# Low halves of the node tiles and of the first weight on GpSimd, transposes by DMA, in a two-layer graph network kernel

## The chip, the core and the metric

The kernel runs on one core of one Trainium2 chip. The metric is the device time of one execution in microseconds. Before the change the median of three runs is 846.42 us (845.54 to 846.95).

## What is computed

1250 nodes with 768 features and 41250 edges (sorted by destination, self loops among them). A graph convolution with a residual and a layer norm comes first, then two attention layers, then a last norm:

```
edge_index = jnp.stack([src, dst])
x = _layernorm(x + _L0_gnn_ref(x, edge_index, L0_gnn_W, L0_gnn_b), axis=-1)
x = _layernorm(x + _L1_gnn_ref(x, edge_index, ...), axis=-1)

def _L0_gnn_ref(x, edge_index, W, b):
    ...
    deg = jax.ops.segment_sum(jnp.ones_like(dst, dtype=x.dtype), dst, num_segments=n)
    norm = deg_inv_sqrt[src] * deg_inv_sqrt[dst]
    h = x @ W
    msg = h[src] * norm[:, None]
    out = jax.ops.segment_sum(msg, dst, num_segments=n)
    return out + b
```

The change touches only how `h = x @ W` of the first layer gets its operands.

## The kernel before

**Tiles and stages.** Nodes lie in T = 10 tiles of 128, features in KD = 6 pieces of 128. Every engine has its own program with semaphores by name; nothing is planned at run time but the number of loop rounds. The stages follow each other: keys of the edges (to about 18 us), counting (to about 129 us), aggregation of the first layer, then the attention layers. The change lies in the counting stage.

**Counting.** The adjacency matrix is built as counts, in NB = 80 blocks of 16 destination nodes. For a block VectorE makes one-hot matrices of six edge tiles (`one_hots`, L1376 for the low part of the source, L1377 for the key) in one of four ring slots; TensorE multiplies them (`count_block`, six matmuls at L819) into one of three PSUM slots, after `open_block` (L806) has begun the slot with the self loops. ScalarE (ACT) copies a finished block out twice (L1113, and L1114, which appears as L1078, the line of its helper `cast`) and gives the slot back with `blk_free`. Every eight blocks VectorE shifts the keys (L1396) and takes low counts (L1385), and TensorE sums degrees (L830).

**The node product between the blocks.** f32 products are made of f16 halves: high times high, low times high, high times low (`node_parts`, L764, two matmuls of 512 and 256 columns for each). Behind block b the function `first_nodes` (b below 18) does pieces of node tiles 0 and 1: in blocks 0 to 5 those that need no low weight, in blocks 6 to 11 it waits for `w_lo` of piece b - 6. From block 18 on, 43 of the 62 blocks carry one piece of tiles 2 to 9 (`project_nodes`); tile 2 begins at block 19, tile 3 at 28, and each later one some nine blocks on. The last five pieces come behind the blocks.

**How the operands are made.** Tile t of x lies in SBUF in f32. TensorE transposes its six pieces (`transposes`, L725) into PSUM; ACT casts them to the high half (`xt_high`), VectorE subtracts that from PSUM for the low half (`xt_low`, L1355). For tiles 2 to 9 this happens at the blocks of FETCH: 13, 19, 28, 37, 45, 54, 63 and 71 (VectorE four blocks later). Of the first weight ACT casts 64 times the rows (`weights`, through L1078) and VectorE makes the low half in one instruction (L1275), one behind each odd block below 12.

**Queues.** SP loads edges, x and the weight at the start, and then waits for the whole node product (`h_done`). GpSimd makes constants until about 8 us and then waits for the last block.

**What GpSimd and VectorE do elsewhere, where the rows below come from.** GpSimd multiplies by a constant (L610 of 128 elements, L640 of 1024), copies (L652), subtracts (L658), and takes a power of one element a partition for the norms: at L636 VectorE waits for it before L1450, at L672 VectorE goes on with L1615, an operation of two SBUF inputs.

Of the kernel before, what the change touches and what calls it, by code (L numbers as in the profile page):

```python
# [17 lines left out]
P = 128  # L18
# [31 lines left out]
FETCH_LAG = 4  # L50
# [10 lines left out]
def done_block(t):  # L61

    return next(b for b in range(NB) if pieces_until(b) >= (t + 1) * KD)


FETCH = {done_block(t) + 2: t + 2 for t in range(T - 2)}
# [56 lines left out]
def gnn_program(nc, x, src, dst, W0, b0, W1, a_src1, a_dst1, b1, g1, be1, Wr1, br1,  # L123
# [7 lines left out]
    with ExitStack() as ctx:  # L131
# [103 lines left out]
        w0_lo = at(195 * KB, [KD, D], f16)  # L235
        src_i = at(156 * KB, [EG, P], i32)
# [119 lines left out]
        def everywhere(row):  # L356
# [7 lines left out]
            x_in0 x_in1 x_in2 x_in3 x_in4 x_in5 x_in6 x_in7 x_in8 x_in9 x_tr xt_hi_ok xt_lo_ok h_done h_read hs_hi_ok hs_lo_ok  # L364
# [65 lines left out]
        def _(sp):  # L430
# [18 lines left out]
            for t in range(T):  # L449
                if t == 2:  # L450
                    weights(0)
                if t < T - 1:
                    sp.dma_start(x_sb[:, t, :], x[t * P:(t + 1) * P, :]).then_inc(S[f"x_in{t}"], 16)
                else:
                    sp.wait_ge(S["pads"], 3)
                    sp.dma_start(x_sb[0:LAST, t, :], x[t * P:N, :]).then_inc(S[f"x_in{t}"], 16)
            sp.wait_ge(S["h_done"], T)
# [130 lines left out]
        def _(pool):  # L588
# [30 lines left out]

            def param(name, row, slot, n=HC):  # L620
                pool.dma_start(par_rows[:, slot, 0:n], everywhere(row)).then_inc(S[name], 16)
# [76 lines left out]
        def _(pe):  # L698
# [18 lines left out]
            def transposes(t):  # L717

                pe.wait_ge(S[f"x_in{t}"], 16)
                if t >= 2:  # L720
                    pe.wait_ge(S["h_read"], t - 1)
                else:
                    pe.wait_ge(S["ident_ok"], 4)
                for k in range(KD):
                    last = pe.transpose(p_out[t % 2][:, k * P:(k + 1) * P], x_sb[:, t, k * P:(k + 1) * P], ident)  # L725
                last.then_inc(S["x_tr"], 1)
# [63 lines left out]
            def project_nodes(t, k, counted=False):  # L790

                if k == 0:
                    pe.wait_ge(S["xt_lo_ok"], t + 1)
                last = node_parts(t, k, NODE_PARTS, counted)
                if k == KD - 1:
                    last.then_inc(S["h_done"], 1)
# [43 lines left out]
            for b in range(NB):  # L840
# [12 lines left out]
                if b in FETCH:  # L853
                    transposes(FETCH[b])
# [221 lines left out]
        def _(act):  # L1076
            def cast(out_, in_, signal, scale=1.0):
                act.activation(out_, in_, ACT.Copy, scale=scale).then_inc(signal, 1)  # L1078
# [8 lines left out]
            def xt_high(t):  # L1087

                act.wait_ge(S["x_tr"], t + 1 if t < 2 else t + 3)
                cast(xt_hi[:, :, t * P:(t + 1) * P], p_out[t % 2].rearrange("p (k n) -> p k n", k=KD), S["xt_hi_ok"])  # L1090

# [5 lines left out]
            def node_evict(t):  # L1097

                act.wait_ge(S["h_done"], t + 1)
                cast(h_sb[:, t, :], p_out[t % 2], S["h_read"], 1 / WSCALE)  # L1100
# [8 lines left out]
            for b in range(NB):  # L1109
# [5 lines left out]
                if b in FETCH:  # L1115
                    xt_high(FETCH[b])
# [149 lines left out]
        def _(dve):  # L1266
# [84 lines left out]
            def xt_low(t):  # L1351

                dve.wait_ge(S["xt_hi_ok"], t + 1)
                cols = slice(t * P, (t + 1) * P)
                dve.tensor_tensor(xt_lo[:, :, cols], p_out[t % 2].rearrange("p (k n) -> p k n", k=KD), xt_hi[:, :, cols],  # L1355
                                  ALU.subtract).then_inc(S["xt_lo_ok"], 1)

# [29 lines left out]
            for b in range(NB):  # L1387
# [4 lines left out]
                if b % 2 == 1 and b < 2 * KD:  # L1392
                    weights(0, [b // 2])
# [3 lines left out]
                if b - FETCH_LAG in FETCH:  # L1397
                    xt_low(FETCH[b - FETCH_LAG])
# [463 lines left out]
```

## Time and profile before

| | |
|---|---|
| median of the runs | 846.42 us |
| the profiled execution, its own time | 845.6 us |
| its span, first to last instruction | 843.8 us |
| TensorE matmul (PE) busy | 810.1 us, 96% of the span |
| VectorE (DVE) busy | 671.5 us, 80% |
| ScalarE (ACT) busy | 269.1 us, 32% |
| GpSimd (POOL) busy | 59.6 us, 7% |
| granted clock of TensorE, mean | 0.994 |

Busy time says how full an engine is, not who sets the pace: that is read from the chain that ended last and from the idle time before each group of instructions. Spans of GpSimd are rough. Matmuls overlap, so the pace of TensorE is read from start to start.

### The profile page before, as it was taken

Reading aid. Unit: us, or ns where it says so; the run is one execution under the profiler, and the core shown is the slowest. Engines: PE = TensorE matmul, PEld = TensorE weight load, DVE = VectorE, ACT = ScalarE, POOL = GpSimd, SP = SyncE. Lnnn points to the kernel's source line nnn. Section 1 sums busy time; section 2 is a strip of 40 time slices with the busy share of each in tenths; the row PEclk is TensorE's granted clock in tenths of the full one; section 3 lists DMA queues with packets and bytes.
Section 4 is the critical chain, followed back from the end, with each engine's and each line's share of the span. In section 5 each row is a group of like instructions: output and inputs, shape, how many; then the busy total and the mean of one; then the engine's idle time right before and its main releaser. Section 6 shows DMA issues by size and latency. Waiting matters only on the chain.

```text
span 843.8 us, 13751 instructions
## 1 busy us (share of the span) xinstructions
PE 810.1 (96%) x5022; PEld 535.6 (63%) x5022; DVE 671.5 (80%) x1181; ACT 269.1 (32%) x510; POOL 59.6 (7%) x81
## 2 busy tenths in 40 slices
PE   5899998999999999999999998999999999999995
PEld 4577774665554444447888887886666666655553
DVE  7999985777566659999988889969873197996686
ACT  3544446010011201015555455643301107760000
POOL 3000002011003000000000000011110000001111
PEclk9999999999999999999999999999999999999998
DMA  8000004041132343226112104113213342212232
GB/s 308 4 2 2 2 3 169 25 162 57 45 156 69 100 163 140 82 104 216 52 68 82 56 1 137 57 63 125 88 64 94 120 134 75 71 57 75 75 113 71
DMA packets 24588, 73.55 MB, mean 87 GB/s; under 512 B 2756, under 2 KB 3756, under 8 KB 24398
## 3 DMA queue, kind: packets, MB, share of 16 engines
q1 hardware_dynamic: 23262, 67.61, 23.0%
q0 software_dynamic: 1264, 5.11, 1.8%
q8 instruction: 39, 0.64, 0.3%
q14 instruction: 23, 0.19, 0.1%
HBM read 52.40 MB, written 20.31 MB: 86 GB/s over the span
## 4 chain that ended last, share of the span: by engine, by line
PE 80%; DVE 11%; issue 3%; DMA 2%; DVEq 2%; ACT 1%; SPq 0%; POOL 0%; POOLq 0%
PE psum L963 19%; PE psum L990 19%; PE psum L1071 12%; PE psum L752 10%; PE psum L878 8%; DVE arena L1463 6%; PE psum L764 6%; PE psum L819 3%; PE psum L978 1%; PE psum L1004 1%; DVEq L1365 1%; PE psum L915 1%; DMA arena<-as_scratch 1%; ACT arena L1078 1%; PE psum L725 1%
## 5 line engine op out<-in xcount | busy, mean ns | idle before, releaser
L990 PE MATMUL psum<-arena 128*128 128x257 f32 x800 | 175.4, 381 | 3.0 <-DVE arena L1607 2.0
L1078 ACT ACTIVATE arena<-psum 128x160 f16<-128x160 f32 (+6 forms) x188 | 94.0, 528 | 261.8 <-PE psum L752 74.0
L990 PEld LDWEIGHTS psum<-arena 128*128 128x128 f32 x800 | 151.2, 190 | 26.7 <-ACT arena L1078 2.7
L752 PE MATMUL psum<-arena 128*128 128x512 f16 x720 | 161.0, 382 | 2.4 <-DVE arena L1435 2.1
L963 PE MATMUL psum<-arena 128*128 128x512 f16 x960 | 158.5, 326 | 0.2 <-ACT arena L1078 0.2
L963 PEld LDWEIGHTS psum<-arena 128*128 128x128 f16 x960 | 93.5, 98 | 62.3 <-ACT arena L1078 0.5
L752 PEld LDWEIGHTS psum<-arena 128*128 128x128 f16 x720 | 70.6, 99 | 85.8 <-issue 5.1
L1071 PE MATMUL psum<-arena 128*128 128x512 f16 (+2 forms) x600 | 98.4, 326 | 0.0
L1071 PEld LDWEIGHTS psum<-arena 128*128 128x128 f16 x600 | 58.3, 97 | 39.8
L1463 DVE CUSTOM_DVE_ANT_0 arena<-arena 128x1280 bf16<-128x1280 bf16 x50 | 71.0, 1488 | 14.3 <-DMA arena<-as_scratch 8.5
L1181 ACT ACTIVATE arena<-arena 128x640 f32<-128x640 f32 x80 | 64.6, 836 | 50.1 <-DVE arena L1592 49.7
L1607 DVE SCALAR_TENSOR_TENSOR arena<-arena 128x640 f32<-128x640 f32 x80 | 65.4, 819 | 15.2 <-ACT arena L1181 9.2
L1078 ACT ACTIVATE arena<-arena 128x768 f16<-128x768 f32 (+4 forms) x58 | 45.7, 809 | 88.4 <-DMA arena<-in_L_gnn_Wr_dram 43.7
L1592 DVE SCALAR_TENSOR_TENSOR arena<-arena 128x640 f32<-128x640 f32 x80 | 70.1, 878 | 0.6 <-DMA arena<-uv_scratch 0.6
L878 PE MATMUL psum<-arena 128*128 128x512 f16 (+1 forms) x400 | 66.7, 326 | 2.7 <-DVE arena L1418 1.9
L764 PE MATMUL psum<-arena 128*128 128x512 f16 x360 | 68.5, 325 | 0.1
L878 PEld LDWEIGHTS psum<-arena 128*128 x400 | 38.3, 98 | 30.8 <-issue 6.2
L1377 DVE TENSOR_TENSOR arena<-arena 128x960 f16<-128x960 int16 x80 | 52.7, 659 | 0.0
L819 PE MATMUL psum<-arena 128*128 128x160 f16 x480 | 46.5, 233 | 3.4 <-DVE arena L1377 2.9
L1376 DVE TENSOR_TENSOR arena<-arena 128x768 f16<-128x768 int16 x80 | 44.7, 559 | 2.0 <-PEq L837 1.2
L819 PEld LDWEIGHTS psum<-arena 128*128 128x128 f16 x480 | 36.5, 97 | 13.6 <-DVE arena L1377 6.9
L1473 DVE CUSTOM_DVE_ANT_0 arena<-psum,arena 128x256 bf16<-128x256 f32 x80 | 28.3, 421 | 20.9 <-PE psum L752 20.9
(173 smaller groups left out, 713.7 us busy)
## 6 DMA issues: line engine op xcount, KB each, us to landing
arena<-in_L_gnn_W_dram SPq DMA_DIRECT2D x22, 384.0 KB, 3.4
r_scratch<-arena SPq DMA_DIRECT2D x10, 512.0 KB, 2.6
arena<-uv_scratch SPq DMA_DIRECT2D x16, 320.0 KB, 4.3
arena<-r_scratch SPq DMA_DIRECT2D x10, 512.0 KB, 3.7
x_scratch<-arena SPq DMA_DIRECT2D x10, 384.0 KB, 4.5
arena<-x_scratch SPq DMA_DIRECT2D x10, 384.0 KB, 3.5
r_scratch<-arena SPq DMA_DIRECT2D x10, 384.0 KB, 2.6
arena<-r_scratch SPq DMA_DIRECT2D x10, 384.0 KB, 3.8
```

Of the source, the lines that this page charges most:

```text
L752: ins = pe.matmul(o[:, a:b], part[:, k, ds(t * P, P)], w[:, k, a:b], start=(not begun and k == 0 and n == 0 and m == 0), stop=(k == kn - 1 ...
L764: last = pe.matmul(p_out[t % 2][:, a:b], part[:, k, t * P:(t + 1) * P], w[:, k, a:b], start=(k == 0 and name == "hh"), stop=(k == KD - 1 a ...
L819: last = pe.matmul(o, ring_lo[slot][:, i // 2, :, i % 2], ring_key[slot][:, i // 2, :, i % 2], start=False, stop=False, skip_group_check=True)
L878: ins = pe.matmul(p_out[par][:, a:b], counts, part[:, k, a:b], start=(not low and k == 0 and n == 0), stop=(not low and k == T - 1 and n = ...
L963: ins = pe.matmul(o[:, a:b], part[:, k, :], w[k][:, a:b], start=(k == 0 and n == 0 and m == 0), stop=(k == KH - 1 and n == 1))
L990: last = pe.matmul(p_att[:, ATT_BANKS[ch][j], 0:HID + 1], pf[n % PSLOTS][:, j * P:(j + 1) * P], xl[ch % H][:, k, 0:HID + 1], start=(k == 0 ...
L1071: last = pe.matmul(p_att2[c % 2][:, j, a:b], p[n][:, t % C1 * P:(t % C1 + 1) * P], xl2[:, k, a:b], start=(k == 0 and m == 0), stop=(k == T ...
L1078: act.activation(out_, in_, ACT.Copy, scale=scale).then_inc(signal, 1)
L1181: act.activation(ee[s], ee[s], ACT.Exp, bias=as_s[:, ch % H, k:k + 1]).then_inc(S["ex_ok"], 1)
L1463: dve.tensor_tensor_reduce(out=out_, in0=mask, in1=row, scale=1.0, scalar=NEG_BIG, op0=ALU.add, op1=ALU.max, accum_out=mx[:, col, t:t + 1] ...
L1592: dve.scalar_tensor_tensor(ee[s], u_row, asd[:, ch % H, k:k + 1], v_row, ALU.add, ALU.max).then_inc(S["larger_ok"], 1)
L1607: dve.scalar_tensor_tensor(pf[n % PSLOTS], ee[s], 1.0, CT[:, k, ds(ch // H * W1C, W1C)], ALU.min, ALU.mult).then_inc(S["pf_ok"], 1)
```

## The change

ACT casts tiles 2 to 9 to their high halves in SBUF, not yet transposed (`x_high`, at blocks 2, 5, 8, ... 23, into one of three slots). GpSimd subtracts for the low halves, also in SBUF. SP issues a DMA transpose for each half of each tile into `xt_hi` and `xt_lo`. GpSimd also makes the low halves of the first weight, in two instructions a row: it multiplies the row by 64 in place, then subtracts the high half. TensorE's transposes and VectorE's subtractions for these tiles, and VectorE's low halves of the first weight, go. New waits: ACT's `x_high` from tile 5 on waits until both halves of tile t - 3 have landed, GpSimd's steps wait for the casts, SP's transposes for GpSimd and ACT, `project_nodes` for the landings and for the eviction of tile t - 2.

```diff
--- before.py
+++ after.py
@@ -47,7 +47,6 @@
 TAIL = 1
 PACK = 10
 HELD = 5
-FETCH_LAG = 4
 HS_FIRST = 3
 
 
@@ -63,7 +62,8 @@
     return next(b for b in range(NB) if pieces_until(b) >= (t + 1) * KD)
 
 
-FETCH = {done_block(t) + 2: t + 2 for t in range(T - 2)}
+SPLIT_X = {2 + 3 * i: i + 2 for i in range(T - 2)}
+XSLOTS = 3
 G_SHIFT = 18
 G_INVERSE = -(-2 ** G_SHIFT // G)
 EG = -(-ET // P)
@@ -233,6 +233,8 @@
         xt_lo = at(110 * KB, [KD, NP], f16)
         w0_hi = at(186 * KB, [KD, D], f16)
         w0_lo = at(195 * KB, [KD, D], f16)
+        x_hi = [at((177 + 3 * i) * KB, [D], f16) for i in range(XSLOTS)]
+        x_lo = [at((177 + 3 * i) * KB + 1536, [D], f16) for i in range(XSLOTS)]
         src_i = at(156 * KB, [EG, P], i32)
         dst_i = at(156 * KB + 1536, [EG, P], i32)
         hi_i = at(159 * KB, [EG, P], i32)
@@ -361,7 +363,7 @@
         S = {n: sem(n) for n in """
             pads src_in dst_in iotas ident_ok keys_prep keys_tr tile_rows ranges_f ranges_t ranges_i key_shift
             keys_ready0 keys_ready1 keys_ready2 keys_ready3 keys_free0 keys_free1 keys_free2 keys_free3 blk_done blk_free
-            x_in0 x_in1 x_in2 x_in3 x_in4 x_in5 x_in6 x_in7 x_in8 x_in9 x_tr xt_hi_ok xt_lo_ok h_done h_read hs_hi_ok hs_lo_ok
+            x_in0 x_in1 x_in2 x_in3 x_in4 x_in5 x_in6 x_in7 x_in8 x_in9 x_tr xt_hi_ok xt_lo_ok x_hi_ok x_lo_ok xt_in0 xt_in1 w_scaled h_done h_read hs_hi_ok hs_lo_ok
             w_in0 w_in1 w_in2 w_in3 w_in4 w_in5 w_hi w_lo clo_ok deg_done dinv_ok over_ok flag_done flag_ok
             neg_tr neg_ok gcn_done gcn_read gcn_var gcn_rstd x1_ok x1_out
             x1_tr x1t_hi_ok x1t_lo_ok as_ok as_tr as_rows as_dram asr0 asr1 max_ok
@@ -454,6 +456,13 @@
                 else:
                     sp.wait_ge(S["pads"], 3)
                     sp.dma_start(x_sb[0:LAST, t, :], x[t * P:N, :]).then_inc(S[f"x_in{t}"], 16)
+            for t in range(2, T):
+                if t >= 4:
+                    sp.wait_ge(S[f"xt_in{t % 2}"], 32 * (t // 2 - 1))
+                for half, made in ((xt_hi, "x_hi_ok"), (xt_lo, "x_lo_ok")):
+                    sp.wait_ge(S[made], t - 1)
+                    sp.dma_start_transpose(half[:, :, t * P:(t + 1) * P],
+                                           (x_hi if half is xt_hi else x_lo)[t % XSLOTS]).then_inc(S[f"xt_in{t % 2}"], 16)
             sp.wait_ge(S["h_done"], T)
             weights(1)
             for t in range(T):
@@ -617,6 +626,17 @@
             pool.tensor_scalar(not_first, ident[:, 0:1], -1.0, None, ALU.add).then_inc(S["br1_ok"], 1)
             pool.memset(half, -0.5).then_inc(S["half_ok"], 1)
 
+            for k in range(KD):
+                pool.wait_ge(S[f"w_in{k}"], 16)
+                pool.wait_ge(S["w_hi"], k + 1)
+                pool.tensor_scalar(wst0[k], wst0[k], WSCALE, None, ALU.mult).then_inc(S["w_scaled"], 1)
+                pool.wait_ge(S["w_scaled"], k + 1)
+                pool.tensor_tensor(w0_lo[:, k, :], wst0[k], w0_hi[:, k, :], ALU.subtract).then_inc(S["w_lo"], 1)
+            for t in range(2, T):
+                pool.wait_ge(S[f"x_in{t}"], 16)
+                pool.wait_ge(S["x_hi_ok"], t - 1)
+                pool.tensor_tensor(x_lo[t % XSLOTS], x_sb[:, t, :], x_hi[t % XSLOTS], ALU.subtract).then_inc(S["x_lo_ok"], 1)
+
             def param(name, row, slot, n=HC):
                 pool.dma_start(par_rows[:, slot, 0:n], everywhere(row)).then_inc(S[name], 16)
 
@@ -717,10 +737,7 @@
             def transposes(t):
 
                 pe.wait_ge(S[f"x_in{t}"], 16)
-                if t >= 2:
-                    pe.wait_ge(S["h_read"], t - 1)
-                else:
-                    pe.wait_ge(S["ident_ok"], 4)
+                pe.wait_ge(S["ident_ok"], 4)
                 for k in range(KD):
                     last = pe.transpose(p_out[t % 2][:, k * P:(k + 1) * P], x_sb[:, t, k * P:(k + 1) * P], ident)
                 last.then_inc(S["x_tr"], 1)
@@ -790,7 +807,8 @@
             def project_nodes(t, k, counted=False):
 
                 if k == 0:
-                    pe.wait_ge(S["xt_lo_ok"], t + 1)
+                    pe.wait_ge(S["h_read"], t - 1)
+                    pe.wait_ge(S[f"xt_in{t % 2}"], 32 * (t // 2))
                 last = node_parts(t, k, NODE_PARTS, counted)
                 if k == KD - 1:
                     last.then_inc(S["h_done"], 1)
@@ -850,8 +868,6 @@
                     for q in range(pieces_until(b - 1), pieces_until(b)):
                         project_nodes(q // KD, q % KD, counted)
                         counted = False
-                if b in FETCH:
-                    transposes(FETCH[b])
                 assert not counted
                 if j == SUBS - 1 and 1 <= t <= T - TAIL:
                     degrees(t - 1)
@@ -1086,8 +1102,15 @@
 
             def xt_high(t):
 
-                act.wait_ge(S["x_tr"], t + 1 if t < 2 else t + 3)
+                act.wait_ge(S["x_tr"], t + 1)
                 cast(xt_hi[:, :, t * P:(t + 1) * P], p_out[t % 2].rearrange("p (k n) -> p k n", k=KD), S["xt_hi_ok"])
+
+            def x_high(t):
+
+                act.wait_ge(S[f"x_in{t}"], 16)
+                if t - XSLOTS >= 2:
+                    act.wait_ge(S[f"xt_in{(t - XSLOTS) % 2}"], 32 * ((t - XSLOTS) // 2))
+                cast(x_hi[t % XSLOTS], x_sb[:, t, :], S["x_hi_ok"])
 
             def xt_rest(t):
 
@@ -1096,6 +1119,10 @@
 
             def node_evict(t):
 
+                if t == T - XSLOTS:
+                    act.wait_ge(S["x_lo_ok"], T - 2)
+                    for i in range(2):
+                        act.wait_ge(S[f"xt_in{i}"], 32 * (T // 2 - 1))
                 act.wait_ge(S["h_done"], t + 1)
                 cast(h_sb[:, t, :], p_out[t % 2], S["h_read"], 1 / WSCALE)
 
@@ -1112,8 +1139,8 @@
                 counted = p_c[b % CSLOTS].rearrange("p (k j) -> p k j", k=T)
                 act.activation(CT[:, :, b * WD:(b + 1) * WD], counted, ACT.Copy)
                 cast(c_hi[:, :, b * WD:(b + 1) * WD], counted, S["blk_free"])
-                if b in FETCH:
-                    xt_high(FETCH[b])
+                if b in SPLIT_X:
+                    x_high(SPLIT_X[b])
                 for n in range(T - 1):
                     if done_block(n) == b:
                         node_evict(n)
@@ -1348,13 +1375,6 @@
             dve.wait_ge(S["dve"], steps_done(1))
             dve.scalar_tensor_tensor(packed, g_tiles, float(1 << PACK), first_up, ALU.mult, ALU.add).then_inc(S["ranges_i"], 1)
 
-            def xt_low(t):
-
-                dve.wait_ge(S["xt_hi_ok"], t + 1)
-                cols = slice(t * P, (t + 1) * P)
-                dve.tensor_tensor(xt_lo[:, :, cols], p_out[t % 2].rearrange("p (k n) -> p k n", k=KD), xt_hi[:, :, cols],
-                                  ALU.subtract).then_inc(S["xt_lo_ok"], 1)
-
             dve.wait_ge(S["dve"], steps_done())
             dve.wait_ge(S["ranges_i"], 1)
             r0, r1 = dve.alloc_register("dve_first"), dve.alloc_register("dve_end")
@@ -1389,13 +1409,9 @@
                 if t and j == 0:
                     dve.wait_ge(S["key_shift"], t)
                 one_hots(b)
-                if b % 2 == 1 and b < 2 * KD:
-                    weights(0, [b // 2])
                 if j == SUBS // 2 and t + 1 < T:
                     dve.wait_ge(S["blk_done"], t * SUBS)
                     dve.tensor_scalar(key_s[(t + 1) % 2], key_s[t % 2], float(-P), None, ALU.add).then_inc(S["key_shift"], 1)
-                if b - FETCH_LAG in FETCH:
-                    xt_low(FETCH[b - FETCH_LAG])
                 if j == SUBS // 2 + 2 and 1 <= t <= T - TAIL:
                     low_counts(t - 1)
             for t in range(T - TAIL, T):
```

## Rows read from the trace of the kernel before

**Rows 1.** The page, part 4: the chain, share of the span by engine.

```profile
PE 80%; DVE 11%; issue 3%; DMA 2%; DVEq 2%; ACT 1%; SPq 0%; POOL 0%; POOLq 0%
```

**Rows 2.** Windows: start:end, length, busy us of each engine, clock, DMA share, GB/s.

```profile
18.00:47.00 29.00, 25.65 (x241) 17.61 (x240) 28.34 (x51) 16.02 (x46) 0.00 (x0) 1.00 0.12 39
47.00:129.00 82.00, 81.73 (x876) 64.18 (x877) 77.06 (x143) 40.63 (x139) 0.53 (x1) 1.00 0.01 2
```

**Rows 3.** Waits of TensorE, 18 to 47 us: total us, times, longest us.

```profile
PE psum L819 <- DVE arena L1377: 2.9, 7, 0.6
```

**Rows 4.** Timeline of VectorE, counting stage: start us, us, what.

```profile
30.77 0.56 DVE L1376 TENSOR_TENSOR arena<-arena 128x768 f16<-128x768 int16 x1
...
31.80 0.56 DVE L1376 TENSOR_TENSOR arena<-arena 128x768 f16<-128x768 int16 x1
```

**Rows 5.** Timeline of TensorE, behind 47 us.

```profile
95.00 0.82 PE L725 MATMUL psum<-arena 128*128 128x128 f32 x6
...
95.65 0.59 PE L819 MATMUL psum<-arena 128*128 128x160 f16 x6
...
100.14 0.23 PE L806 MATMUL psum<-arena 128*128 128x160 f16 x1
...
101.62 0.23 PE L806 MATMUL psum<-arena 128*128 128x160 f16 x1
```

**Rows 6.** Timeline of TensorE: blocks 0, 11, 16, 17; degrees; counts of block 24.

```profile
19.89 0.81 PE L764 MATMUL psum<-arena 128*128 128x512 f16 x4
...
36.80 0.82 PE L764 MATMUL psum<-arena 128*128 128x512 f16 x4
...
44.38 0.81 PE L764 MATMUL psum<-arena 128*128 128x512 f16 x4
...
45.52 0.81 PE L764 MATMUL psum<-arena 128*128 128x512 f16 x4
...
53.99 0.64 PE L830 MATMUL psum<-arena 128*128 128x1 f16 x20
54.60 0.60 PE L819 MATMUL psum<-arena 128*128 128x160 f16 x6
```

**Rows 7.** Groups by line, VectorE, 18 to 136: busy us, mean ns | idle us.

```profile
L1355 DVE TENSOR_TENSOR arena<-psum,arena 128x768 f16<-128x768 f32 x8 | 7.7, 962 | 1.3 <-ACT arena L1078 1.2
L1275 DVE SCALAR_TENSOR_TENSOR arena<-arena 128x768 f16<-128x768 f32 x6 | 5.7, 955 | 0.0
```

**Rows 8.** Timeline, GpSimd's elementwise work, and ACT's first cast of the weight.

```profile
5.65 0.62 POOL L610 TENSOR_SCALAR arena<-arena 128x128 f16<-128x128 f16 x1
...
16.99 0.84 ACT L1078 ACTIVATE arena<-arena 128x768 f16<-128x768 f32 x1
...
209.41 2.79 POOL L640 TENSOR_SCALAR arena<-arena 2x1024 f32<-2x1024 f32 x1
...
255.05 1.03 POOL L652 CAST arena<-arena 2x1024 f16<-2x1024 f32 x1
...
257.83 1.26 POOL L658 TENSOR_TENSOR arena<-arena 2x512 f16<-2x512 f32 x1
```

**Rows 9.** By source line: count, ns min/median/max, first and last start.

```profile
L636 POOL TENSOR_TENSOR arena<-arena x10: 537/542/543, 149.7 to 208.9; 128x1 f32<-128x1 f32 x10
L672 POOL TENSOR_TENSOR arena<-arena x10: 1512/1514/1534, 484.0 to 629.4; 128x1 f32<-128x1 f32 x10
L1615 DVE SCALAR_TENSOR_TENSOR arena<-arena x10: 1274/1276/1277, 483.8 to 629.2; 128x1024 f32<-128x1024 f32 x10
L1450 DVE TENSOR_SCALAR arena<-arena x10: 679/680/1395, 150.2 to 209.5; 128x768 f32<-128x768 f32 x10
L1288 DVE SCALAR_TENSOR_TENSOR arena<-arena x1: 558/558/558, 5.9 to 5.9; 128x384 f32<-128x384 int32 x1
```

**Rows 10.** The page, part 6, DMA issues: KB each, median us to landing.

```profile
r_scratch<-arena SPq DMA_DIRECT2D x10, 512.0 KB, 2.6
...
x_scratch<-arena SPq DMA_DIRECT2D x10, 384.0 KB, 4.5
```

## The prediction

> **What bounds the kernel now.** I read the page first. TensorE owns 80% of the chain that ended last, VectorE 11% [rows 1]. So time is won only where TensorE gets less to do or waits less. The change touches the counting stage alone, from about 18 to 129 us, so the windows come next: up to 47 us VectorE is full (28.34 of 29.00) and TensorE isn't (25.65); from 47 to 129 TensorE is full (81.73 of 82.00) and VectorE has air (77.06). GpSimd has 0.53 us to do in all of it [rows 2].
>
> Who waits for whom splits the stage in two. Up to 47 us TensorE waits seven times for the one-hots of L1377, 2.9 us in all; behind that, to 128.7 us, the view has no row for it [rows 3]. The timeline shows why. VectorE makes the one-hots of a block in 1.03 us (30.77 to 31.80) [rows 4], with a weight's low half (L1275, 0.96 us [rows 7]) beside every second block. TensorE, where nothing holds it, needs 1.14 us for an early block: six counts (L819), one opening (L806), four node matmuls (44.38 to 45.52) [rows 6]. A later block with a node piece takes 1.48 us (opening at 100.14 to opening at 101.62) [rows 5]. So the part up to block 17 is VectorE's, the part behind it TensorE's. The landmarks, by node matmuls: block 0 at 19.89, block 11 at 36.80, block 17 at 45.52; the counts of block 24 at 54.60 [rows 6].
>
> **What is removed.** TensorE loses 8 groups of six transposes. One takes 0.65 us (95.00 to the next L819 at 95.65) [rows 5]; seven lie behind block 17, on TensorE's full part: 7 x 0.65 = 4.5 us gained for certain. The eighth is in block 13. VectorE loses 8 x 0.96 (L1355) and 6 x 0.96 (L1275), 13.4 us [rows 7]. Behind 47 us that gains nothing, since TensorE is full there; before it, it would let TensorE run at its 1.14 us a block: from 19.89, block 11 would start at 32.4 and block 17 at 39.9 (with one degree group, L830, of 0.6 us: 53.99 to 54.60 [rows 6]), 5.6 us sooner than now. ACT makes eight high halves from SBUF (0.84 us a cast [rows 8]) instead of from PSUM: nothing.
>
> **What takes its place.** GpSimd gets 12 instructions for the weight, then 8 for node tiles 2 to 9, in program order. The weight's low halves are due at blocks 6 to 11, one per block: `first_nodes` waits for `w_lo`, and counts, openings and everything else on TensorE queue behind that wait. The price of one comes from GpSimd's rows [rows 8]: the multiplication took 0.62 us for 128 elements and 2.79 for 1024, so 2.42 ns an element and 2.17 us for 768; the subtraction took 1.26 us for 512, so 1.74 (same rate plus the 0.3 us start that L610 leaves over) to 1.89 (in proportion) for 768, taken as 1.80. With 0.08 us between dependent ones a weight row costs 2.17 + 0.08 + 1.80 + 0.08 = 4.13 us, against TensorE's 1.14 us a block. ACT's first cast of the weight ends at 17.83 (16.99 + 0.84) [rows 8], so low half 0 comes at 21.9 and low half 5 at 21.9 + 5 x 4.13 = 42.5.
>
> GpSimd does not run alone. The same one-element power takes 0.54 us at L636, where VectorE waits for it, and 1.51 us at L672, where VectorE has just begun a two-input operation of 1.28 us [rows 9]: GpSimd waited some 0.97 us, three quarters of it. One-hot instructions come every 0.5 us [rows 4], so each GpSimd instruction waits some 0.4 us while VectorE is busy: the first five or so (2 us). Once TensorE is held and VectorE's ring of four is full, VectorE works 1 us in 4, which gives 0.1 us for each of the rest. I add 3 us (bounds 0 and 12 x 0.4 = 4.8): low half 5 at 45.5. Block 11 starts then, 8.7 us later than now.
>
> **The second hold is ACT's.** At block 11 ACT is to write the high half of tile 5 into the slot of tile 2, and waits until both halves of tile 2 are transposed. The low half of tile 2 stands behind the weight on GpSimd: 45.5 + 2.1 = 47.6. Then a DMA transpose. No such transfer is in this trace; the plain ones of 384 to 512 KB land in 2.6 to 4.5 us [rows 10], and one half is 192 KB, so I take 3.5: 51.1. Behind ACT's wait stand the evictions of blocks 12 and later, and TensorE can open only three blocks ahead of them. It counts blocks 12, 13 and 14 (to 48.9), then stands until ACT has cast tile 5 (0.84) and evicted block 12 (0.5): 52.4. So 3.5 us more are lost. Tile 3 lands at about 53.2, as ACT comes to it. Blocks 14 to 17 follow at 1.14 and one degree group at 0.6: block 17 at about 56.5, against 45.52 now: 11.0 us late.
>
> **The transposes** sit on SP's queue, behind the loads and ahead of the second weight, which waits for `h_done` anyway. A tile needs two, and its turn comes every three blocks. The 62 blocks behind 47 us take 82 - 4.5 = 77.5 us, 1.25 each, so a turn is 3.75 us: hidden as long as one half costs under 1.9 us of queue and transfer. No row prices that; bounds are nothing (only landing counts, and they overlap) and the whole 2.6 to 4.5 us of landing, one behind the other. I take the hidden end, since plain transfers overlap, and keep the other as rival B. Tile 2 is first needed by TensorE at block 19, tile 3 at block 28: no wait there.
>
> **The sum.** +11.0 at block 17, -4.5 behind it: +6.5 us. VectorE behind 47 us has 77.06 - 7 x 0.96 = 70 us of work [rows 2, 7], under TensorE's 77.5: no new bound. The profiled execution took 845.6 us (span 843.8 and 1.8 around it), so 852.1; the median of the runs is 0.8 us higher: **853**. With no mutual wait and transposes landing in 2 us it would be 848; with 0.5 us of wait each and transposes in 7 us, 859. That is the forecast's own range.
>
> **Rivals.** *A: GpSimd shuts VectorE out.* The other direction of the wait: each GpSimd instruction holds what VectorE's one-hots need. For it: L1450, 0.68 us in all but one place, took 1.40 us beside L640, 0.72 us more [rows 9]. Against it: that L640 ran 2.79 us and did not hold L1450 for all of it, and L1288, two inputs of 384 elements beside L610, took 0.56 us, no more than L1615's 1.28 for 1024 lets one expect (0.48 and a start) [rows 9]. At 0.72 each, VectorE loses 20 x 0.72 = 14 us, most of it while it would stand idle anyway, so the forecast holds. If the whole instruction is shut out, VectorE loses, up to block 24, 6 x 2.17 + 13 x 1.80 = 36.4 us and is rid of 8 instructions of 0.96: its one-hots come 36.4 - 7.7 = 28.7 us late, TensorE with them, and only six transposes (3.9) are saved behind: +24.8, 871 us. It decides once a GpSimd instruction costs VectorE some 1 us: then 19 - 7.7 is over the 11.0 us that TensorE is late anyway. The Trainium skill (SBUF — State Buffer, Who interferes with whom) has just this rule: of a GpSimd instruction that reads SBUF and a VectorE one with two SBUF inputs, the later one blocks fully until the first ends. The wait at L672 agrees, the 0.72 us at L1450 doesn't.
>
> *B: the transposes are slow.* Nothing in the trace speaks to it either way but the plain transfers [rows 10]. ACT's turns at blocks 14, 17, 20 and 23 each wait for the tile three before. If a half costs 3.5 us in series, a tile takes 7.0 against a turn of 3.75: 4 x 3.25 = 13 us more, 866. The Trainium skill (VectorE: DVE Perf Modes, The three transpose paths) gives 1309 ns for a 128x128 transpose by DMA; if the six of a half ran in series, that would be 7.9 us a half. Another of its pages (Advanced Engine Details and Errata, X-Bar Transpose) calls such transfers as fast as plain ones, which would leave the sum as it is. No run here shows either.
>
> *C: faster.* If GpSimd's multiplication ran as fast as its copy of 1024 elements (1.03 us at L652) [rows 8], a weight row would cost 2.8 us, low half 5 come at 34.5, tile 2 land at 40, block 17 start where it does now, and the end be 4.5 us sooner: 842. With all of it hidden, block 17 comes at 39.9 and the gain is 5.6 + 4.5 = 10 us: 836. Against it: for as many elements on the same two partitions the multiplication L640 took 2.79 us.
>
> *D: no change to measure.* GpSimd somewhat faster than its rows, small holds: gain and loss within 1.7 us.
>
> **How the numbers follow.** Forecast (848 to 859) 0.43; A, 862 to 874, 0.24; B, 857 to 880, 0.12; C, 835 to 844, 0.15; D 0.06. A measurement of this kernel can tell about 0.2%, 1.7 us. Faster: C, 0.15. Same: D and a little of the forecast's low end, 0.10. Slower: the rest, 0.75. The range of 8 in 10 runs from 843, leaving out most of C, to 873, leaving out the ends of A and B.
>
> **What would show it.** GpSimd's rows for the new lines: about 2.2 and 1.8 us, or longer by the wait. Node matmuls of block 11 near 45.5, with the idle time before them ended by GpSimd; if by L1377, rival A, and L1376 would be longer than its 0.56 us [rows 4]. ACT's wait at block 11 should be ended by a DMA, with TensorE idle 3 to 4 us; such waits at 14 to 23 as well mean rival B. Behind block 24 the stage should take some 4 us less than now. TensorE's clock was granted in full, 1.00, in this stage [rows 2]; should the holds lower it, that adds to the time. The prediction fails low if GpSimd takes under 1.5 us an instruction, and high if VectorE is shut out.

## The result, and the profile of the changed kernel

| | before | after |
|---|---|---|
| median of the runs, us | 846.11 (845.54 to 846.95, 4 runs) | 858.45 (855.96 to 858.97, 4 runs) |
| ratio, 95% interval | | 1.0139 [1.0117, 1.0162] |
| the profiled execution, us (span) | 845.6 (843.8) | 858.01 (855.9) |

The changed kernel is 1.4% slower. Forecast: 853, range 843 to 873. Between the two profiled executions lie 12.4 us, where the sum had 6.5.

First its page, parts 1 and 4, against [rows 1]: VectorE's share of the chain rose by one point, TensorE's share is what it was.

```profile
PE 807.5 (94%) x4974; PEld 532.1 (62%) x4974; DVE 683.4 (80%) x1167; ACT 268.5 (31%) x510; POOL 114.5 (13%) x101
...
PE 80%; DVE 12%; issue 3%; DVEq 2%; DMA 1%; ACT 1%; POOL 0%; SPq 0%; POOLq 0%
```

Then the windows of the counting stage (columns as in [rows 2]; the order is TensorE, its weight loads, VectorE, ACT, GpSimd, clock):

```profile
18.00:47.00 29.00, 17.78 (x150) 12.08 (x149) 28.81 (x28) 12.96 (x34) 28.50 (x14) 0.97 0.17 50
47.00:100.00 53.00, 47.44 (x489) 35.21 (x487) 52.98 (x86) 24.50 (x82) 26.36 (x7) 0.92 0.34 56
100.00:141.00 41.00, 41.00 (x457) 31.83 (x453) 35.79 (x67) 18.74 (x69) 1.02 (x2) 1.00 0.01 2
```

Up to 47 us VectorE is as full as before (28.81 of 29.00), but gets 28 instructions done where it did 51 [rows 2]. Fewer instructions in the same busy time: they have become longer. The groups by line, 18 to 141 us (busy us, mean ns, then idle time before them and who ended it), say which:

```profile
L1397 DVE TENSOR_TENSOR arena<-arena 128x960 f16<-128x960 int16 x80 | 58.9, 736 | 0.0
...
L1396 DVE TENSOR_TENSOR arena<-arena 128x768 f16<-128x768 int16 x80 | 58.2, 728 | 2.9 <-PE psum L837 1.5 <-PEq L855 1.2
L837 PE MATMUL psum<-arena 128*128 128x160 f16 x480 | 47.5, 237 | 16.1 <-DVE arena L1397 15.7 <-issue 0.2
...
L638 POOL TENSOR_TENSOR arena<-arena 128x768 f16<-128x768 f32 x8 | 30.0, 3759 | 11.7 <-ACT arena L1094 11.7
...
L632 POOL TENSOR_SCALAR arena<-arena 128x768 f32<-128x768 f32 x6 | 14.5, 2422 | 10.1 <-ACT arena L1094 10.1
...
L634 POOL TENSOR_TENSOR arena<-arena 128x768 f16<-128x768 f32 x6 | 10.5, 1755 | 0.5
```

L1396 and L1397 are the one-hots (L1376 and L1377 before). L1396 takes 728 ns in the mean, where one alone takes 0.56 us [rows 4]; the two groups took 97.4 us before and take 117.1 now, 19.7 us more. With two smaller groups (L1405, L1414, 1.4 and 1.3 us more) it is 22.4 us. TensorE's waits, over the same stretch (total us, times, longest), follow:

```profile
ACT arena L1094 <- DMA arena<-arena: 4.9, 1, 4.9
...
PE psum L837 <- DVE arena L1397: 15.7, 11, 3.2
...
PE psum L781 <- POOL arena L634: 0.7, 1, 0.7
```

15.7 us for VectorE's one-hots (2.9 before [rows 3]), 0.7 us for GpSimd's low halves of the weight. Two timelines, GpSimd's and then VectorE's over the same four microseconds, show how one instruction of GpSimd lengthens one of VectorE:

```profile
35.08 2.43 POOL L632 TENSOR_SCALAR arena<-arena 128x768 f32<-128x768 f32 x1
37.59 1.66 POOL L634 TENSOR_TENSOR arena<-arena 128x768 f16<-128x768 f32 x1
39.23 2.43 POOL L632 TENSOR_SCALAR arena<-arena 128x768 f32<-128x768 f32 x1
```

```profile
35.45 1.27 DVE L1397 TENSOR_TENSOR arena<-arena 128x960 f16<-128x960 int16 x1
36.64 0.55 DVE L1396 TENSOR_TENSOR arena<-arena 128x768 f16<-128x768 int16 x1
37.11 0.65 DVE L1397 TENSOR_TENSOR arena<-arena 128x960 f16<-128x960 int16 x1
37.68 2.00 DVE L1396 TENSOR_TENSOR arena<-arena 128x768 f16<-128x768 int16 x1
39.59 1.27 DVE L1397 TENSOR_TENSOR arena<-arena 128x960 f16<-128x960 int16 x1
```

Beside the multiplication (L632, one input) L1397 takes 1.27 instead of 0.65 us: 0.62 lost. Beside the subtraction (L634, two inputs) L1396 takes 2.00 instead of 0.55: 1.45 lost, nearly all of the subtraction's 1.66. In the 4.15 us of a weight row VectorE makes the one-hots of two blocks, 2.08 us each instead of 1.03. Where a block's chain of matmuls opens (L806 before, L824 after; from the timelines of TensorE) the account of the stage can be read:

| opening of block | before | after | late by |
|---|---|---|---|
| 12 | 36.48 | 42.52 | 6.0 |
| 15 | 41.35 | 54.48 | 13.1 |
| 18 | 45.45 | 59.24 | 13.8 |
| 24 | 52.95 | 68.37 | 15.4 |
| 79 | 126.30 | 137.81 | 11.5 |

### The profile page after: what moved, and what is told of

Read it like the earlier page. It is cut to its first block, busy times and chain, and to the rows that moved or that the text cites. A ratio compares the mean times of both kernels' runs of the same rounds, so it can differ in the third digit from the quotient of the medians.

```text
span 855.9 us, 13698 instructions
## 1 busy us (share of the span) xinstructions
PE 807.5 (94%) x4974; PEld 532.1 (62%) x4974; DVE 683.4 (80%) x1167; ACT 268.5 (31%) x510; POOL 114.5 (13%) x101
## 4 chain that ended last, share of the span: by engine, by line
PE 80%; DVE 12%; issue 3%; DVEq 2%; DMA 1%; ACT 1%; POOL 0%; SPq 0%; POOLq 0%
PE psum L979 18%; PE psum L1006 18%; PE psum L1087 11%; PE psum L769 11%; PE psum L894 8%; DVE arena L1479 6%; PE psum L781 6%; PE psum L837 4%; DVE arena L1397 1%; PE psum L994 1%; PE psum L1020 1%; DVEq L1385 1%; DMA arena<-as_scratch 1%; PE psum L931 1%; PE psum L848 1%
## 5 line engine op out<-in xcount | busy, mean ns | idle before, releaser
L1094 ACT ACTIVATE arena<-psum 128x160 f16<-128x160 f32 (+6 forms) x180 | 87.5, 516 | 260.3 <-PE psum L769 79.3
L1094 ACT ACTIVATE arena<-arena 128x768 f16<-128x768 f32 (+3 forms) x66 | 52.4, 813 | 91.8 <-DMA arena<-in_L_gnn_Wr_dram 42.1
L837 PE MATMUL psum<-arena 128*128 128x160 f16 x480 | 47.5, 237 | 16.1 <-DVE arena L1397 15.7
L1396 DVE TENSOR_TENSOR arena<-arena 128x768 f16<-128x768 int16 x80 | 58.2, 728 | 2.9 <-PE psum L837 1.5
L1397 DVE TENSOR_TENSOR arena<-arena 128x960 f16<-128x960 int16 x80 | 58.9, 736 | 0.0
L692 POOL TENSOR_TENSOR arena<-arena 128x1 f32<-128x1 f32 x10 | 15.2, 1516 | 304.0 <-DVE arena L1445 304.0
```

What stands on the lines that cost most here:

```text
L837: last = pe.matmul(o, ring_lo[slot][:, i // 2, :, i % 2], ring_key[slot][:, i // 2, :, i % 2], start=False, stop=False, skip_group_check=True)
L1397: dve.tensor_tensor(ring_key[slot], key_io[b % SUBS].unsqueeze(1).to_broadcast([P, GP, T * WD, 2]), pairs(keys, T * WD), ALU.is_equal).the ...
```

## The experiments

Each kernel changes one thing in the kernel before or in the changed one; ratios are against the kernel before. The expectations call the theories by letters. P is the port, a name for whatever the two engines share: VectorE pays for each instruction of GpSimd, 1.45 us for a subtraction and 0.62 for a multiplication. L is the forecast's own chain: what counts is when GpSimd has the weight's low halves. S is the prediction's second hold, ACT at the slot of a node tile. Q, R, T and V came up in the course of the runs, on what lets GpSimd in and keeps it out.

**Tiles alone.** The weight's low halves go back to VectorE.

```diff
-            for k in range(KD):
-                ...
-                pool.tensor_tensor(w0_lo[:, k, :], wst0[k], w0_hi[:, k, :], ALU.subtract).then_inc(S["w_lo"], 1)
             for t in range(2, T):
...
                 one_hots(b)
+                if b % 2 == 1 and b < 2 * KD:
+                    weights(0, [b // 2])
```

> Half of the change: node tiles as in the changed kernel, the weight's low halves back on VectorE (one instruction behind each odd block below 12). Theory P (the shared port: a GpSimd subtraction shuts VectorE out for about 1.45 us, a GpSimd multiplication for about 0.6): VectorE loses 8 x 1.45 = 11.6 us to the tiles' subtractions and is rid of 8 x 0.96 = 7.7, so block 24 is about 4 us late and 4 us come back behind it: 846 to 848, TensorE waiting on the one-hots, not on GpSimd. Rival L (GpSimd's results just come late, whatever VectorE does): nothing is due early any more, 841 to 843. Rival S (ACT's wait for the slot of tile 2 is what costs): the tiles' chain starts at 26 us instead of 43, so that wait is gone: 853 less nothing else, i.e. 853.

Measured 855.06 us, 1.0099 [1.0073, 1.0125]. P (846 to 848) and L (841 to 843) missed; S had 853, but with ACT's wait for the slot gone, and that wait is longer than in the changed kernel, so its mechanism missed too. GpSimd's timeline, and the waits of 18 to 141 us, show something new:

```profile
24.97 24.69 POOL L632 TENSOR_TENSOR arena<-arena 128x768 f16<-128x768 f32 x3 [17.04 <-ACT arena L1088]
```

```profile
ACT arena L1088 <- DMA arena<-arena: 12.1, 1, 12.1
DVE arena L1390 <- PE psum L831: 11.7, 8, 8.9
...
PE psum L818 <- ACT arena L1088: 10.5, 1, 10.5
```

The first three subtractions, 5 us of work, took 24.7 us. VectorE's instructions in that time were as short as before (0.55, 0.65, 0.95 us) and stood back to back from 24.97 to 44.97; the first subtraction was over at 46.5, 1.5 us after VectorE had stopped, its ring of one-hots full because TensorE stood still. So it is GpSimd that was shut out here, for 20 us. ACT meanwhile waited 12.1 us for the slot of tile 2, TensorE 10.5 us for ACT.

**The weight alone**, added to the kernel before.

```diff
+            for k in range(KD):
+                ...
+                pool.tensor_scalar(wst0[k], wst0[k], WSCALE, None, ALU.mult).then_inc(S["w_scaled"], 1)
+                pool.wait_ge(S["w_scaled"], k + 1)
+                pool.tensor_tensor(w0_lo[:, k, :], wst0[k], w0_hi[:, k, :], ALU.subtract).then_inc(S["w_lo"], 1)
...
                 one_hots(b)
-                if b % 2 == 1 and b < 2 * KD:
-                    weights(0, [b // 2])
```

> The other half alone: the weight's low halves on GpSimd, the node tiles as before. Theory P: VectorE loses 6 x (1.45 + 0.62) = 12.4 us and is rid of 6 x 0.96 = 5.7: block 12 some 6.7 us late and nothing given back, 852 to 854. Rival L: GpSimd's row of 4.15 us sets blocks 6 to 11, low half 5 at 43.4 instead of 36.8: 852 to 853 as well, but with TensorE's waits ended by GpSimd and the one-hots no longer than before. Rival S: no slots here, 846.

Measured 852.16 us, 1.0075 [1.0054, 1.0096]; block 79 opens 6.7 us late, and P's arithmetic is 6 x (1.45 + 0.62) - 6 x 0.96 = 6.7. The chain of low halves comes to the same: node matmuls of block 11 at 43.47, as against 36.80 [rows 6], is 6.7 us too. The waits up to 47 us, 8.9 for VectorE's one-hots and 0.7 for GpSimd, say that VectorE set the pace of the blocks and that the chain was only just the later of the two at the last one. By its time alone this run can't tell P from L.

**Six slots for the tiles**, in the changed kernel.

```diff
-XSLOTS = 3
+XSLOTS = 6
...
-        x_hi = [at((177 + 3 * i) * KB, [D], f16) for i in range(XSLOTS)]
-        x_lo = [at((177 + 3 * i) * KB + 1536, [D], f16) for i in range(XSLOTS)]
+        x_hi = [at((168 + 3 * i) * KB, [D], f16) for i in range(XSLOTS)]
+        x_lo = [at((168 + 3 * i) * KB + 1536, [D], f16) for i in range(XSLOTS)]
```

> The changed kernel with six slots for the untransposed halves instead of three: ACT's cast of tile 5 at block 11 no longer waits for the transposes of tile 2; only tiles 8 and 9 wait for a slot at all. Theory P: TensorE's 3.2 us idle at block 13 was ended by one-hots that the subtractions shut out, not by ACT, so 857 to 859. Rival S: ACT's 4.9 us wait was the loss, 853 to 854.

Measured 857.85 us, 1.0144 [1.0121, 1.0167], as slow as the changed kernel's 1.0139. ACT's wait of 4.9 us is gone from the trace, and TensorE waits 17.3 us for L1397 instead of 15.7:

```profile
PE psum L837 <- DVE arena L1397: 17.3, 10, 4.3
```

The second hold was there and cost nothing: VectorE's one-hots came as late anyway.

**Tiles alone, six slots.** The same edit on the first experiment.

> The run with the tiles alone on GpSimd, with six slots instead of three. There ACT stood 12.1 us at block 11 for the slot of tile 2 and TensorE 10.5 us behind it, while GpSimd's first subtraction waited from 25.0 to about 44.8 us, until VectorE had filled its ring and stopped. Theory Q: the hold moves to block 19, where TensorE needs tile 2 itself: VectorE runs to block 22 or so (about 43 us), stops, the subtractions for tile 2 need 1.6 us and the transposes 2.8 more; TensorE is at block 19 at 46.6, so the hold shrinks to 2 to 5 us: 844 to 850. Theory P without shutting out: 846 to 848, no hold of TensorE, subtractions of 2 to 3 us. If the slots play no part: 855.

Measured 851.81 us, 1.0068 [1.0046, 1.0091], 3 us better than with three slots but short of what was expected. GpSimd's row, and the waits:

```profile
25.21 37.77 POOL L632 TENSOR_TENSOR arena<-arena 128x768 f16<-128x768 f32 x7 [17.27 <-ACT arena L1088]
```

```profile
PE psum L775 <- DMA arena<-arena: 8.4, 1, 8.4
```

VectorE now ran on to 51 us, GpSimd stayed out until then, and it was TensorE's own wait for the transposed tile 2 that brought the stop (8.4 us at block 19). The slots only move the place: the tile is late because GpSimd is shut out.

**No GpSimd.** ACT's high halves and the DMA transposes stay, the low halves are VectorE's again. Two spacings of the tiles; in the first they come at blocks 9, 16, 25, 34, 42, 51, 60 and 68, in the second at 12, 19, ..., 61.

```diff
-SPLIT_X = {2 + 3 * i: i + 2 for i in range(T - 2)}
+SPLIT_X = {12 + 7 * i: i + 2 for i in range(T - 2)}
...
-            for k in range(KD):
-                ...
-            for t in range(2, T):
-                ...
...
+            def x_low(t):
+                dve.wait_ge(S["x_hi_ok"], t - 1)
+                dve.tensor_tensor(x_lo[t % XSLOTS], x_sb[:, t, :], x_hi[t % XSLOTS], ALU.subtract).then_inc(S["x_lo_ok"], 1)
...
                 one_hots(b)
+                if b % 2 == 1 and b < 2 * KD:
+                    weights(0, [b // 2])
+                if b - 4 in SPLIT_X:
+                    x_low(SPLIT_X[b - 4])
```

> Nothing on GpSimd: the tiles' low halves are subtracted by VectorE in SBUF, four blocks behind ACT's casts, the casts moved to blocks 9, 16, 25, 34, 42, 51, 60 and 68; the weight on VectorE; the transposes by DMA as in the changed kernel. All theories: TensorE is rid of its transposes and VectorE has what it had, so 7 x 0.65 = 4.5 us less than before, 841 to 842. Should the DMA transposes cost something of their own, or the late casts hold ACT, it would be 844 or more.

Measured 847.2 us, 1.0011 [0.9996, 1.0026]: no change. Up to block 69 it led by 2.6 us (opening at 110.60 against 113.22), and lost that and 1.1 us more at blocks 72 to 75: the eviction of tile 7 waits for the low half of every tile (`T - XSLOTS`), and the last one was made only at block 72.

> As the run with the low halves on VectorE, but ACT's casts at blocks 12, 19, 26, ... 61, so that tile 9's halves are transposed long before ACT's eviction of tile 7 at block 69 waits for them. In the run before, blocks 27 to 69 took 3.1 us less than in the kernel before (five groups of transposes, 3.25 expected), and 3.7 us went at blocks 72 to 75 where ACT waited. Theory (DMA transposes cost nothing of their own, that wait was all): 841 to 842.5. Rival (the transposes' transfers slow something else later on): 845 or more.

Measured 842.99 us (11 runs, 841.82 to 843.99), 0.9965 [0.9953, 0.9977]: 0.35% faster than before, and the best kernel here. Block 79 opens at 123.23, 3.1 us sooner. Its waits, 18 to 141 us:

```profile
PEld psum L827 <- DVE arena L1392: 11.4, 20, 1.2
...
PE psum L827 <- DVE arena L1392: 4.9, 11, 1.0
```

None is on a transpose. TensorE is rid of eight groups of 0.65 us [rows 5], 5.2 in all, and waits 2.0 us more for VectorE's one-hots (4.9, 2.9 before [rows 3]): 3.2 us, and block 79 has 3.1. The high halves, slots and transposes are those of the changed kernel, except for the blocks at which ACT casts; that spacing with GpSimd at work was not run. What GpSimd's instructions cost by themselves is what the next runs show.

**Fourteen spare subtractions on GpSimd**, in the kernel before: P by itself, with nobody waiting for the results but one late eviction.

```diff
+            pool.wait_ge(S["x_in0"], 16)
+            pool.wait_ge(S["x_in1"], 16)
+            pool.wait_ge(S["w_hi"], 1)
+            for i in range(14):
+                ...
+                pool.tensor_tensor(spare[i % 3], x_sb[:, 0, :], x_sb[:, 1, :], ALU.subtract).then_inc(S["spare"], 1)
```

> The kernel before, with 14 spare subtractions on GpSimd (two SBUF inputs, 128x768, results used by nobody) from the first cast of the weight on. Nothing waits for them. Theory P in its first form (each gets its turn between two of VectorE's instructions and shuts VectorE out for 1.45 us): 14 x 1.45 = 20 us more in VectorE's stretch, 862 to 866. Theory Q (GpSimd's subtraction gets in only where VectorE pauses, as in the run with the tiles alone, where it stood from 25.0 to about 44.8): VectorE hardly pauses before 125 us, so the subtractions last up to tens of us and cost 0 to 5 us: 846 to 851. Rival L: 846.

Measured 866.84 us, 1.0252 [1.0228, 1.0276]: 21 us for 14, 1.5 us each. That is P; Q, by which GpSimd gets in only where VectorE pauses, had 846 to 851. VectorE's timeline:

```profile
22.35 2.16 DVE L1387 TENSOR_TENSOR arena<-arena 128x768 f16<-128x768 int16 x1
24.43 2.25 DVE L1388 TENSOR_TENSOR arena<-arena 128x960 f16<-128x960 int16 x1
26.61 2.56 DVE L1286 SCALAR_TENSOR_TENSOR arena<-arena 128x768 f16<-128x768 f32 x1
...
44.32 1.93 DVE L1407 TENSOR_SCALAR arena<-arena 128x648 int16<-128x648 int16 x1
```

Strictly one of GpSimd's, one of VectorE's, and each of VectorE's is 1.6 us longer, the weight's low half (0.95 alone) and a shift with one input (0.32 alone) too.

**Fourteen spare multiplications** (`pool.tensor_scalar(spare[i % 3], x_sb[:, 0, :], WSCALE, None, ALU.mult)` in their place).

> The same with 14 spare multiplications by a constant (one SBUF input, 128x768 f32). Theory P: 0.62 us of VectorE each, 8.7 us, all in VectorE's stretch of 18 to 47 us: 853 to 855. Theory Q: as the subtractions, shut out, 846 to 849. Rival L: 846.

Measured 854.82 us, 1.0105 [1.0083, 1.0128]: 9.2 us for 14, 0.65 each (block 79 opens 8.8 us late, 0.63 each), close to the 0.62 read from the changed kernel's timeline. Together they took GpSimd 30.44 us, 2.17 each.

**Six spare subtractions, at four places.** Is it who comes first that decides whether GpSimd is let in (R), or what it reads (T)? Six from 18 us on; the same from 23 us, into a VectorE that hasn't paused (`S["w_hi"], 6`); these with an f16 second input (`w0_hi[:, 0, :]`); and f32 again from block 30 (`S["blk_done"], 30`), where TensorE is the bound.

> The kernel before with six spare subtractions on GpSimd from the first cast of the weight on (about 18.0 us, while VectorE stands still before its first one-hots at 18.2). Theory P and theory R (whoever comes while the other holds the port without a pause waits for a pause; once GpSimd is in, its chain and VectorE's instructions take turns): six turns, VectorE's first six instructions last 2.0 to 2.2 us, 6 x 1.5 = 9 us more, about 855. Rival L: 846.

> The same six subtractions, but from the last cast of the weight on (about 23.2 us), when VectorE runs without a pause. One line differs. Theory P: the same 9 us, 855. Theory R: GpSimd is shut out for as long as VectorE doesn't pause, tens of us (VectorE's first real pause in the kernel before is behind 100 us, where it waits for ACT and for its ring), its row of the first subtraction is that long, and VectorE's one-hots keep 0.55 and 0.65 us until then; from 100 us on VectorE has some slack, so the time is 846 to 850.

> As the run with six spare subtractions from 23 us, but the second input is an f16 tile (the weight's high half) in place of an f32 one, as in the changed kernel. Theory T (the kind of operand decides whether a lone GpSimd subtraction gets in between two of VectorE's back-to-back instructions: with an f16 input it waits for a pause): the first subtraction lasts tens of us, the one-hots keep 0.55 and 0.65 us, 846 to 849. Theory P (every one gets its turn): six turns again, 853 to 855.

> The six spare subtractions with f32 inputs, but started at block 30 (about 61 us), where TensorE sets the pace and VectorE's instructions still follow each other closely. Theory P: six turns of 1.5 us, 9 us of VectorE's time; VectorE is 2 blocks ahead there and its ring holds 4, and it has 5 us of air in the rest of the stage, so half of it shows: 849 to 852. Theory V (how early VectorE is in its stretch, or the phase, decides who gets in): a first subtraction of 10 us or more, as in the changed kernel at 70 us, and 846 to 848.

Measured 853.8, 854.33, 854.02 and 854.12 us; ratios 1.0093 [1.0071, 1.0114], 1.0106 [1.0084, 1.0128], 1.0097 [1.0068, 1.0126] and 1.01 [1.007, 1.013]. GpSimd's row, from the four kernels in turn:

```profile
18.01 12.81 POOL L627 TENSOR_TENSOR arena<-arena 128x768 f16<-128x768 f32 x6 [10.08 <-ACT arena L1087]
```

```profile
23.07 12.64 POOL L627 TENSOR_TENSOR arena<-arena 128x768 f16<-128x768 f32 x6 [15.14 <-ACT arena L1087]
```

```profile
23.56 31.67 POOL L627 TENSOR_TENSOR arena<-arena 128x768 f16<-128x768 f32 x6 [15.63 <-ACT arena L1087]
```

```profile
61.85 13.60 POOL L627 TENSOR_TENSOR arena<-arena 128x768 f16<-128x768 f32 x6 [53.93 <-PE psum L815]
```

R falls with the second: VectorE was running back to back, and the first subtraction got in at once (L1388 at 23.19 took 2.26 us). With the f16 input it stayed out for 20 us, until 43.8. T expected a faster kernel from that, and there it missed. VectorE's timeline of the third kernel shows why:

```profile
43.31 0.65 DVE L1388 TENSOR_TENSOR arena<-arena 128x960 f16<-128x960 int16 x1
43.88 0.95 DVE L1366 TENSOR_TENSOR arena<-psum,arena 128x768 f16<-128x768 f32 x1
44.74 1.14 DVE L1387 TENSOR_TENSOR arena<-arena 128x768 f16<-128x768 int16 x1
45.80 2.09 DVE L1388 TENSOR_TENSOR arena<-arena 128x960 f16<-128x960 int16 x1
```

L1366 reads one input from PSUM, the other from SBUF. The subtraction gets in beside it: the trace has its end at 45.46, and less the 1.64 us that one takes alone it began at 43.8, as L1366 did (an estimate). L1366 keeps its 0.95 us, and L1387 behind it pays only 0.59. From there the two engines alternate: shut out first, the six cost the same 8 us later. In the fourth kernel it happens likewise at the L1366 at 63.09: the first subtraction ends at 64.85, 1.81 us after 63.0. There TensorE was the bound, P expected 849 to 852 and V, by which an early or late moment in the stretch decides, 846 to 848; the 854.12 is above both, and block 79 opens 10.2 us late. VectorE had 4.9 us of air up to 129 us [rows 2], but spread over all blocks; the window of the alternation shows VectorE full and TensorE half empty (columns as in [rows 2]):

```profile
62.00:76.00 14.00, 7.47 (x77) 5.23 (x75) 14.00 (x11) 2.90 (x13) 13.45 (x6) 0.83 0.01 2
```

Eleven instructions where the kernel before has 27 in the same window; the ring of four blocks doesn't last that long.

## Why the prediction came out as it did

It named the direction and its range held the time; 858.45 lies even in the forecast's own 848 to 859, at its upper end, and below rival A's 862 to 874. That is luck as far as the mechanism goes: what happened is rival A's, at smaller prices. The profiled executions differ by 12.4 us, the sum by 6.5; the missing 5.9 stand at these steps (the table of openings).

- **GpSimd's prices: right.** At the shortest the multiplication took 2.15 us (2.17 forecast), the subtraction 1.64 (1.80), a weight row 4.15 (4.13).
- **The mutual wait: the step that failed.** The prediction saw it in the rows and laid it on GpSimd, 3 us on the chain of low halves; VectorE it charged with 0.72 us at most and called that time idle. Measured: GpSimd's weight chain ended 2.1 us sooner than forecast (43.4, not 45.5), and VectorE lost 1.45 us to each subtraction and 0.62 to each multiplication, 6 x 0.62 + 14 x 1.45 = 24 us by price, 22.4 by the groups. The 0.72 had been read beside a multiplication (L640), and for multiplications it was near; the fault was to put it on the 14 subtractions too, which cost twice as much. That is rival A's mechanism. Its threshold was stated, "some 1 us" an instruction, and 24 us over 20 instructions is 1.2. Its time of 871 was too high, for a multiplication costs 0.62 where 2.17 was put and a subtraction 1.45 where 1.80 was: up to block 24, 6 x 0.62 + 13 x 1.45 less the 7.7 it is rid of is 14.9 us late, where rival A had 28.7 and the trace has 15.4.
- **"VectorE would stand idle anyway": wrong.** The test the prediction had set was who ends the idle time before block 11's matmuls. GpSimd does, for 0.7 us, as the forecast said; but L1397 ends all eight others up to 47 us, 10.5 us in all, as rival A said. By that one block alone either could be claimed.
- **Block 11 and block 17.** Node matmuls at 43.46 and 59.31, forecast 45.5 and 56.5. So 2.8 us were missing at block 17. ACT's wait for the slot came as forecast, at block 11 and ended by a DMA: 4.94 us, until 48.23. But six slots take it away and gain nothing, so the 3.5 us charged for it were not its price. TensorE stood at the same place for VectorE:

```profile
45.88 0.98 PE L837 MATMUL psum<-arena 128*128 128x160 f16 x6 [1.60 <-DVE arena L1397]
46.66 0.34 PE L824 MATMUL psum<-arena 128*128 128x160 f16 x1
46.79 1.49 PE L781 MATMUL psum<-arena 128*128 128x512 f16 x4
51.48 0.98 PE L837 MATMUL psum<-arena 128*128 128x160 f16 x6 [3.21 <-DVE arena L1397]
```

- **The clock.** Full in this stage before [rows 2]; here the four node matmuls at 46.79 take 1.49 us instead of 0.81, and the window 46 to 56 us below has a granted clock of 0.51, that is the lower level of 1.2 GHz. Ahead of it TensorE had stood idle for 1.6 to 1.7 us at 36.8, 40.9 and 45.9. The prediction named a lower clock as something that would add, and a part of the delay at blocks 14 to 17 is this. How much of the total it is was not separated: VectorE lost time again behind it and may have covered it.

```profile
46.00:56.00 10.00, 6.79 (x35) 4.42 (x35) 10.00 (x12) 3.58 (x9) 4.70 (x3) 0.51 0.71 138
```

- **Blocks 18 to 24: 2.3 us missing.** Forecast was a gain of 0.65; the trace has a loss of 1.6. Three more tiles are subtracted here, and VectorE pays some 1.4 us for each (L1396 at 58.41, 1.90 us, and at 61.04, 2.00 us; L1405 at 64.57, 2.26 us for 0.81). The claim "VectorE behind 47 us is no bound" failed here.
- **Behind block 24: right.** To block 79, 69.44 us instead of 73.35, 3.9 saved by six groups of transposes, to the tenth. The last subtraction, in it, cost VectorE 1.45 us and TensorE nothing.
- **The transposes: right, rival B refuted.** 16 of them, issued in 1.23 us each, landed in 2.8 us (median; 3.5 was taken), and in this kernel no engine waited for one without GpSimd in front of it.
- **What is left:** 0.6 us behind block 79 and 0.3 outside the span, not looked into. 2.8 + 2.3 + 0.6 + 0.3 is 6.0, against the 5.9 sought.
- **The rule against the change.** Two-input instructions block each other for nearly the whole of it, the rows say: VectorE loses 1.45 us to a subtraction of 1.64 (second input f16) and 1.6 to one of 1.81 (both f32), and GpSimd, in the alternation, takes 2.1 to 2.2 us for one of 1.81. The Trainium skill (SBUF — State Buffer, Who interferes with whom) has that rule, and here the trace agrees; for the one-input multiplication, 0.62 of 2.15 us, it doesn't.

Without GpSimd the change would have been rival C's kind: 842.99, found with the low halves on VectorE.

What stays open is what lets a GpSimd instruction in. It went in at once or waited up to 26 us. A stop of VectorE let it in with tiles alone, an instruction with a PSUM input in the third and fourth kernels with six; neither was there in the second (23.07) and in the changed kernel at 83.5, nor at 60.9, where an f16 subtraction got in at once. The order of arrival and the type of the second input don't settle it alone, and no run here separates more.

## What to carry to other kernels

Work that GpSimd takes from VectorE is not free because GpSimd stands idle: here a two-input instruction on SBUF cost VectorE nearly its own length when VectorE's next one had both inputs in SBUF (the one-input shift L1407 paid as much; L1366, with one input in PSUM, paid nothing). 1.45 us lost for 0.96 us saved is a bad trade even where GpSimd itself has nothing else to do. Read such a collision from both sides in the trace, charge it to the busier engine first, and test with a few spare instructions before moving real work. The transposes were the part worth having: transposing 16-bit halves by DMA frees TensorE, if each half is made well before anything that waits in order behind it.

## What the runs showed of the hardware that was not expected

- A lone GpSimd subtraction of 1.64 us can be shut out by back-to-back VectorE instructions for 20 to 26 us (24.97 to 44.8 with tiles alone; 25.2 to 51 with six slots; 23.56 to 43.8 with the f16 input; the ends are estimates, the trace's end of the subtraction less its 1.64 us). In the changed kernel the last one shows as

```profile
70.01 15.10 POOL L638 TENSOR_TENSOR arena<-arena 128x768 f16<-128x768 f32 x1 [3.86 <-ACT arena L1094]
```

  Such a row is not work: while it stands, VectorE's instructions keep their length, until the one at 83.53 takes 2.00 us.
- The price is not the same for all kinds. One input on GpSimd: 0.62 us of 2.15. Two: 1.45 of 1.64 with an f16 input, 1.6 of 1.81 with f32 ones. On VectorE's side the one-input shift L1407 (0.32 to 1.93 us) is held just as two-input ones are, while L1366, which reads one input from PSUM, keeps its 0.95 us with a subtraction beside it.
- A DMA transpose of a 128x768 f16 half within SBUF keeps its queue for 1.23 us and lands in 2.8 us.
